# An attention and mixture-of-experts kernel: biased maxima in two halves of the heads, all first products beside the maxima, and a new order of residual, copy and norm

## What is computed

```python
# attention, per sequence: 32 heads of 8 dims
q, k, v = rope(x @ Wq.T), rope(x @ Wk.T), x @ Wv.T
gate = q . mean of k over each chunk of 32 tokens   # own chunk always, future chunks never
allowed = the 4 best chunks of each query, and causal
p = softmax(where(allowed, q.k * 8**-0.5, -1e30))
o = rmsnorm(p @ v) * o_norm_weight * sigmoid(x @ Wg1.T @ Wg2.T)
x = layernorm(x + o @ Wo.T)
# experts: 2 shared and 16 routed (4 chosen per token), 176 hidden features each
hidden = relu(x @ w1 + b1)
x = layernorm(x + x + sum_e gating_e * (hidden_e @ w2_e + b2_e))
```

## Time and profile before

| | |
|---|---|
| median of three runs | 1453.98 us |
| profiled execution, its own time | 1453.75 us |
| its span, first to last instruction | 1451.7 us |
| PE busy | 1332.4 us (92%) |
| DVE busy | 1087.7 us (75%) |
| ACT busy | 842.7 us (58%) |
| POOL busy | 533.9 us (37%) |
| mean granted clock of PE | 0.961 of full speed |

### The profile page before, as it was taken

One profiled execution on the slowest core, in us unless ns is written; L12 is line 12 of the kernel. 1 busy time (PEld: TensorE's weight loads), 2 busy tenths in 40 slices (PEclk: granted clock), 3 DMA queues, 4 the chain that ended last, 5 costly groups with the idle time before them and its releaser, 6 DMA issues.

```text
span 1451.7 us, 29057 instructions
## 1 busy us (share of the span) xinstructions
PE 1332.4 (92%) x10992; PEld 738.7 (51%) x10992; DVE 1087.7 (75%) x2747; ACT 842.7 (58%) x1266; POOL 533.9 (37%) x638
## 2 busy tenths in 40 slices
PE   5677999999998999999999999989999899999597
PEld 3422475535754366534755356543665347553364
DVE  6994688957897578966889578975889668885434
ACT  5406774396735876277743967358762877439121
POOL 3203542254323642245422553235432454225143
PEclk8667999999999999999999999999999999999799
DMA  6001022200321021210222003210112102220031
GB/s 243 16 15 17 16 79 76 52 17 16 104 66 38 30 59 60 74 31 16 82 71 55 16 17 102 71 33 30 60 62 71 31 16 68 73 53 23 13 113 58
DMA packets 52283, 77.81 MB, mean 54 GB/s; under 512 B 6334, under 2 KB 26800, under 8 KB 51888
## 3 DMA queue, kind: packets, MB, share of 16 engines
q1 hardware_dynamic: 52144, 75.96, 18.0%
HBM read 67.02 MB, written 8.65 MB: 52 GB/s over the span
## 4 chain that ended last, share of the span: by engine, by line
PE 61%; DVE 19%; ACT 11%; DVEq 3%; issue 3%; DMA 2%; POOL 1%; SPq 0%; POOLq 0%
PE PS L562 14%; PE PS L574 13%; PE PS L718 8%; ACT UQ L992 7%; PE PS L492 7%; PE PS L509 3%; DVE hr L1163 3%; ACT UK L992 2%; DVE CM L1356 2%; DVEq L1155 2%; PE PS L773 2%; PE PS L413 2%; DVE CM L1275 2%; PE PS L728 2%; PE PS L483 2%
## 5 line engine op out<-in xcount | busy, mean ns | idle before, releaser
L1051 POOL TENSOR_TENSOR hp<-hr,hp 128x512 f16<-128x512 f32 (+1 forms) x200 | 237.1, 1186 | 584.1 <-ACT hp L849 520.0
L1356 DVE TENSOR_REDUCE CM<-PS 128x32 f32<-128x1024 f32 x320 | 376.2, 1218 | 23.2 <-PE PS L492 18.9
L574 PE MATMUL PS<-W,hp 128*128 128x256 f16 (+1 forms) x2400 | 323.2, 274 | 4.6 <-POOL hp L1051 3.6
L562 PE MATMUL PS<-x1T,W 128*128 128x512 f16 (+1 forms) x1200 | 320.6, 385 | 0.0
L840 ACT ACTIVATE hr<-PS,CF 128x512 f32<-128x512 f32 (+1 forms) x200 | 137.2, 686 | 234.3 <-PE PS L562 234.3
L574 PEld LDWEIGHTS PS<-W,hp 128*128 128x128 f16 (+1 forms) x2400 | 216.9, 98 | 96.1 <-issue 34.7
L849 ACT ACTIVATE hp<-hr 128x512 f16<-128x512 f32 (+1 forms) x178 | 112.5, 632 | 169.3 <-DVE hr L1163 156.2
L1163 DVE TENSOR_TENSOR hr<-hr,gB 128x512 f32<-128x512 f32 x176 | 126.2, 717 | 64.9 <-ACT hr L840 58.5
L992 ACT ACTIVATE UK<-PS 128x1024 f32<-128x1024 f32 x160 | 153.0, 1037 | 11.4 <-PE PS L509 11.0
L562 PEld LDWEIGHTS PS<-x1T,W 128*128 128x128 f16 (+1 forms) x1200 | 107.7, 100 | 100.7 <-issue 34.9
L992 ACT ACTIVATE UQ<-PS 128x1024 f32<-128x1024 f32 x160 | 150.9, 1041 | 3.1 <-PE PS L509 1.4
(11 more groups left out here) (150 smaller groups left out, 1793.8 us busy)
## 6 DMA issues: line engine op xcount, KB each, us to landing
gB<-gates SPq DMA_DIRECT2D x64, 256.0 KB, 3.3
gB<-gates SPq DMA_DIRECT2D x32, 224.0 KB, 2.9
gB<-gates SPq DMA_DIRECT2D x32, 192.0 KB, 2.9
gB<-gates SPq DMA_DIRECT2D x32, 160.0 KB, 2.6
xT<-in_xT SPq DMA_DIRECT2D x8, 512.0 KB, 5.8
qET<-rows SPq DMA_DIRECT2D x16, 256.0 KB, 5.2
v<-in_x SPq DMA_DIRECT2D x8, 512.0 KB, 4.1
gB<-gates SPq DMA_DIRECT2D x32, 128.0 KB, 2.9
```

What stands on the lines that cost most here:

```text
L562: mm = pe.matmul(PS[0:w, BK_H[c % 2], :], W1[:, a, k, bass.ds(f0, w)], x1T[:, e, k, :], start=(n == 0), stop=(n == 5))
L574: mm = pe.matmul(PS[:, BK_Y + j // 2, (j % 2) * D:(j % 2 + 1) * D], hp[0:w, slot, a, j * P:(j + 1) * P], W2[0:w, e, bass.ds(c, 1), :].rear ...
L1051: nc.gpsimd.tensor_tensor(hp[0:w, slot, 1, :], hr[0:w, slot, :], hp[0:w, slot, 0, :], ALU.subtract).then_inc(pool_hp, 1)
L1356: nc.vector.tensor_reduce(dst, src, AX.X, ALU.max).then_inc(dve_cm, 1)
```

## The change

The biased maxima are computed in two halves of the heads. The first half (heads 0 to 15) is done within the maxima stage, behind units 21, 24, 27 and 30 (`FREE`). Its transposes stand behind the third up part of chunk 22, and SP's first half of `bias_rows` stands ahead of the gate broadcast of chunk 24. The second half is done after the maxima stage. Its transposes stand after key unit 8, its copy is made by DVE, and its rows are awaited ahead of key unit 20. All up parts (to chunk 24) are dealt beside the maxima, and so are the output gate's products, now in two calls whose operands stay on one row group each. The downs of chunk 22 (three parts), 23 and 24 stand among the first key units. Chunk 24's relu and high half go from ACT to DVE. The first ten key units use two pairs of banks. On DVE the residual sums, the copy of the outputs of group 0 and the whole norm follow in this order.

```diff
-C_FIRST, C_TOPK, C_MAX, C_BIAS = (0, 3), (3, 11), (11, 22), (22, 25)
+PAIRS = [n % 2 if n < 2 * NU else (2, 0, 1)[(n - 2 * NU) % 3] for n in range(TU)]
+BACK = [next((k for k in range(1, n + 1) if PAIRS[n - k] == PAIRS[n]), 0) for n in range(TU)]
+C_FIRST, C_TOPK, C_MAX, C_LATE = (0, 3), (3, 11), (11, 24), (24, 25)
-DEALT += [(MC - 2, 4), (MC - 2, 5), (MC - 2, 6)]
+DEALT += [(MC, 0), (MC, 1), (MC, 2)]
+AT_SEL, AT_GATE, AT_NEG = (1, 2), (3, 4), 11
+FREE = [u for u in range(TU // 2, MU) if all(part != 2 for _, part in dealt(u - 1))][0:2 * NT:2]
...
+            def bias_rows(b, n):                       # SP
+                pairs = slice(H // 4 * n, H // 4 * (n + 1))
+                if n == 0:
+                    sp.wait_ge(s_sel, 32 * (b + 1))
+                sp.wait_ge(pe_mx, b * TU + TU // 2 * (n + 1) + 1)
...
+                sp.wait_ge((act_neg, dve_neg)[n], b + 1)
...
+                    if m < B - 1 and c == NC - 1:      # in spread_gates
+                        bias_rows(m + 1, 0)
...
+                def gate_half(c, i):                   # PE
+                    r = ROW_G1 * i
+                    for j in range(2):
+                        mm = pe.matmul(PS[:, BK_H[(c + 1) % 2], j * D:(j + 1) * D], g1T[r:r + HD, j * P:(j + 1) * P],
+                                       WG2[r:r + HD, :], start=True, stop=True, tile_position=(r, 0))
+                def maxima_rows(bank, n):
+                    pe.wait_ge(dve_bias, (2 * b + n + 1) * NT)
+                    for j in range(NT):
+                        mm = pe.transpose(PS[0:HALF, bank, j * P:(j + 1) * P], negm[:, j, HALF * n:HALF * (n + 1)], ident)
...
+                    if n < RING:                       # in unit(g, d), n = g * NU + d
+                        pe.wait_ge(dve_cm, (b + 1) * TU + n + 1)
+                    if n == 2 * NU and m is not None:
                         pe.wait_ge(dve_z, 2 * m + 3)
+                    if n == TU // 2:
+                        pe.wait_ge(s_rows[1], 64 * (b + 1))
...
+                pe.wait_ge(s_rows[0], 64 * (b + 1))
+                unit(0, 0)
+                unit(0, 1)
+                late_down(NC - 3, (1,))
+                unit(0, 2)
+                late_down(NC - 3, (2, 3))
+                unit(0, 3)
+                late_down(NC - 2, (0, 1))
+                unit(0, 4)
+                late_down(NC - 2, (2, 3))
+                unit(1, 0)
+                outputs(0, 0, 0)
+                unit(1, 1)
+                late_down(NC - 1, (0, 1))
+                unit(1, 2)
+                outputs(0, 0, 1)
+                late_down(NC - 1, (2, 3))
+                unit(1, 3)
+                maxima_rows(BK_H[1], 1)
+                outputs(0, 0, 2)
+                unit(1, 4)
+                outputs(0, 0, 3)
...
+                        if u in FREE:                  # DVE, in the loop over the units
+                            maxima(FREE.index(u), 0)
+                if m is not None:
+                    dve.wait_ge(pe_h, m * NC + NC)
+                    nc.vector.tensor_scalar(hr[:, s_last, :], PS[:, BK_H[s_last], :], b1[:, NC - 1:NC], 0.0, ALU.add,
+                                            ALU.max).then_inc(s_hid, 1)
+                    gated(m, NC - 1, s_last, split=True)
                 for j in range(NT):
+                    maxima(j, 1)
+                dve.wait_ge(pe_neg, 2 * b + 2)
+                nc.vector.tensor_scalar(negT[:, 1, :], PS[0:HALF, BK_H[1], :], 1.0 / UNIT, None, ALU.mult).then_inc(dve_neg, 1)
...
                 if m is not None:
-                    finish(m, lambda: copy_outputs(0))
-                else:
-                    copy_outputs(0)
+                    residual(m)
+                copy_outputs(0)
+                if m is not None:
+                    finish(m)
```

More of the change, by code:

```diff
@@ L648, in turn @@
                 settled_wait(pe, dve_gm, (b + 1) * 3)
[L649 to L671, removed]
-                        down(m, c, c % 2, j)
[L674 to L705, removed]
+                for u in range(MU):
+                    if u == 1:
+                        pe.wait_ge(act_kz, (b + 1) * NG + 1)
+                        pe.wait_ge(act_eq, (b + 1) * NG + 1)
+                    pe.wait_ge(dve_cm, b * TU + u + 1)
+                    max_unit(u // NU, u % RING, u % NU)
+                    for cc, part in dealt(u):
+                        c = C_MAX[0] + cc
+                        if part == 0 and cc - 1 in AT_SEL:
+                            pe.wait_ge(act_sel, 2 * b + AT_SEL.index(cc - 1) + 1)
+                        if part == 0 and cc - 1 in AT_GATE:
+                            pe.wait_ge(act_eg, 2 * b + AT_GATE.index(cc - 1) + 1)
+                        if part == 0 and cc - 1 == AT_NEG:
+                            pe.wait_ge(act_neg, b + 1)
+                        if m is not None and part < 3:
+                            up(m, c, part)
+                        elif m is not None:
+                            down(m, c, c % 2, part - 3)
+                        if part == 2 and cc in AT_SEL:
+                            selection_rows(c, AT_SEL.index(cc))
+                        if part == 2 and cc in AT_GATE:
+                            gate_half(c, AT_GATE.index(cc))
+                        if part == 2 and cc == AT_NEG:
+                            if m is not None:
+                                pe.wait_ge(s_hid, m * NC + c + 2)
+                            maxima_rows(BK_H[(c + 1) % 2], 0)
@@ L942, in turn @@
                             high(m, c, (C_TOPK[0] + u) % 2)
[L943 to L953, removed]
@@ L1107, in causal @@
                     for n, t in enumerate(KORDER):
+                        if g == 0 and n == 1 and m is not None:
+                            for c in range(*C_LATE):
+                                low(m, c, c % 2)
                         if n != 2:
@@ L1191, in layernorm @@
                 inverse_root(NT)
-                if between is not None:
-                    between()
                 for j in range(NT):
```

133 lines of the change are left out of this document (70 added, 63 removed).

## The result

| | before | after |
|---|---|---|
| median | 1453.95 us (4 runs) | 1489.95 us (4 runs, 1487.41 to 1493.77) |
| ratio to before, 95% interval | | 1.0251 [1.0227, 1.0275] |
| span of the profiled execution | 1451.7 us | 1487.6 us |
| DVE busy | 1087.7 us | 1128.3 us |
| mean granted clock of PE | 0.961 | 0.958 |

The kernel is 36 us slower. The sign is as forecast, but 1463.5 was predicted and the range ended at 1475.

The account below looks back on a forecast made before the run. PE was taken to bound the maxima stage, DVE 4% behind, then ACT the keys. A turn: -11.5 + 8.0 + 1.3 + 4.3 = +2.1 us, seven +14.7, turn 0 -5.1: +9.6 on 1453.75, so 1463.5; range 1445 to 1475.

Parts of the forecast that it names:

- A: Between maxima and key stages: the late stage goes, first exponential at T + 0.43; 11.5 us less per turn.
- T: The moment at which PE leaves the maxima stage of a turn.
- B: PE's maxima stage: moved ups, downs, gate products and transposes add 8.0 us a turn, between 7.1 and 8.2.
- C: Second half of the maxima stage: DVE is 1.9 us too long, PE waits 1.3 a turn, between 0.3 and 2.3.
- a sum or reduction costs 0.16 + 0.001 per element: DVE's first-half maxima in the maxima stage: duration per operation, 3.6 us in all with the added drains.
- the forecast's own sum: Maxima stage, units 20 to 33: DVE 1.9 us too long, less about 0.6 that PE runs ahead; PE waits 1.3.
- D: Key stage: DVE's chain makes the copy of group 1 late; 4.3 us lost a turn, between 2.7 and 5.
- Both holes: Key stage: exponentials stop about 1.7 us by unit 10, for the residual sums, and 2.5 at unit 18.
- The clock: Rival: PE's clock falls after the new key-stage wait, 0.9 us each, at most 1.7; 1470 to 1476; chance 0.18.
- Turn 0: No experts, DVE bounds: first half adds 3.6 us, first exponential about 117.3 instead of 123.02; -5.1 us in all.

Follow-up runs that it names:

- run 7: The changed kernel without the scaled sums and reductions of the first half of the biased maxima, memsets in their place: 1464.88 us, ratio 1.0078.
- run 4: The kernel before with only DVE's order changed to residual sums, copy of group 0, whole norm: 1481.57 us, ratio 1.0191.

## Why the prediction was right in direction and wrong in size

- **A**, the late stage goes: right. First exponential at T + 0.43, 11.5 us.
- **B**, the work moved to PE: right. With DVE out of the way (run 7) the stage is 8.4 longer, forecast 8.0 with 8.2 as the upper bound. The gate's eight products took 2.1 us instead of the 1.06 of the earlier trace rows, with 1.9 forecast. The trace agrees with the case of one row group, and with the rule that the prediction cited from the Trainium skill ("TensorE: Matmul & The Clock Gate", section "The mechanism" of the packing part); no run alternates the row groups in the new place.
- **C**, DVE in the second half of the maxima stage: the step that failed. The place was right (PE waits behind units 24, 27, 30), the size was not: 1.3 forecast, at most 2.3, and 3.2 measured. The failing term is "a sum or reduction costs 0.16 + 0.001 per element". The earlier trace rows has that duration where POOL rests. In the new place each sum starts while POOL makes a low half, and takes 0.53 longer: 2.1 us a turn. With it the forecast's own sum gives 1.9 + 2.1 - 0.6 = 3.4. I had looked at DVE's and PE's totals and never laid POOL's timeline beside them, though both engines follow the same chunk. The trace of the kernel before had the sign, between the very rows that I took the duration from. DVE's and POOL's rows there:

```profile
789.48 0.46 DVE L1365 SCALAR_TENSOR_TENSOR rep<-cbias,CM 128x128 f32<-128x128 f16 x1 [0.44 <-issue]
...
793.43 1.19 DVE L1163 TENSOR_TENSOR hr<-hr,gB 128x512 f32<-128x512 f32 x1 [0.16 <-issue]
```

```profile
788.64 1.16 POOL L1051 TENSOR_TENSOR hp<-hr,hp 128x512 f16<-128x512 f32 x1 [4.16 <-ACT hp L849]
792.91 1.16 POOL L1051 TENSOR_TENSOR hp<-hr,hp 128x512 f16<-128x512 f32 x1 [3.12 <-ACT hp L849]
```

  The sum of 128 elements takes 0.46 beside POOL, where the same one takes 0.29 in turn 0, and the gating takes 1.19 instead of 0.68.
- **D**, the key stage: right in mechanism and nearly in size. Both holes are where they were forecast, and DVE's chain ends at T + 19.87. In part errors cancel in that: the copy of the second half is 0.8 late and the norm 0.4 shorter than forecast. And the first hole is mostly PE's own list (1.26 of 1.93), not the residual sums. In turn 7, where the clock does not fall, the stage takes 1381.36 - 1337.52 = 43.84, 5.0 more than before; forecast 4.3, upper bound 5. The holes are 1.93 + 2.17 = 4.1 of it, and 0.4 more is in the group behind the second one, where PE waits 0.61 for the next copy and five exponentials take 5.11 instead of 4.69.
- **The clock** was a rival at 0.18, an alternative to the forecast, with 0.9 a turn and 1.7 at most. It came on top of D in six turns of seven. Their key stages average 45.2, 1.3 over turn 7, and about 0.2 of this is the longer waits of turns 5 and 6. This was a fault of logic as well: D itself makes the wait of 2.5 us that the rival needs, so with D likely the clock's fall was likely too. The sum had the clock at nothing, and this is the second step that failed.
- **Turn 0**: -5.1 forecast, -2.0 without its earlier start. From first to last reduction DVE takes 54.5 us instead of 48.3: 6.2 more, where 3.6 was forecast. I had given the moved products no cost there since DVE bounds. But PE, with pauses, works there in part at the low clock (0.50 between 80 and 83 us). Its timeline has the second four gate products, and DVE's the reductions behind them:

```profile
80.74 2.07 PE L671 MATMUL PS<-WG,g1T 8*128 8x256 f32 x4
```

```profile
83.93 9.57 DVE L1394 TENSOR_REDUCE CM<-PS 128x32 f32<-128x1024 f32 x8 [1.85 <-PE PS L510]
```

  They take 2.07 instead of 1.12, DVE runs dry for 1.85, and its other waits in the stage sum to 1.7, where it had 0.49 before: 3.0 more. The halves themselves cost the other 3.2. That the slow products make the wait is read from the order of the rows; no run took them out.

A turn by these terms: -11.5 + 8.4 + 3.2 + 5.0 + 1.3 x 6/7 = +6.2, against 5.7 measured. The difference lies in the kernel before, which the terms take from its undisturbed turns. Its key stages of turns 1 and 3 are 0.9 longer than the others, at a clock of 0.96, and the late stage of turn 5 is 1.1 longer, since PE waits 1.58 for `negT` there and not 0.52. That is 2.9 us over seven turns, 0.4 each, which the kernel before loses too and the sum leaves out. The prediction took turn 4 for all turns, as repeating within 1 us; in fact they take 168.1 to 170.0.

The forecast was 26 us short. By these terms C is about 13 of it, the clock 8, D 5, B 3 and turn 0 less than 2, and those 3 us of the kernel before go the other way. Why turn 7 keeps its clock behind an equal wait of 2.47 stays open.

## What to carry to other kernels

When work is moved onto an engine that has room on average, lay the timelines of all engines over the new place, and look at what runs beside each moved operation. Here one unit's shift of four small sums was worth 14 us. An operation that is held up by another engine shows as a longer row, not as idle time, so a list of waits misses it: compare the durations of equal rows. A long chain of vector work should be cut where the matmul engine waits for something behind it. Here that gave back 22.6 of the 28.4 us that leaving the work out gives, and the clock was kept too. And a rival that the forecast's own mechanism sets off belongs in the sum, not beside it.

## What the runs showed of the hardware

A scaled sum on DVE with both inputs in SBUF (`cbias` and `CM`, L1378) does not get through its elements while POOL's subtraction runs. It took 0.89 us beside it and 0.36 behind it, for the same 192 elements. The four sums of the maxima stage end 0.09, 0.15, 0.21 and 0.28 us after POOL's operation, about 0.001 per element: only their start is hidden. The masks on POOL (L1137) hold a sum too. DVE's and POOL's rows behind T in turn 4:

```profile
816.14 1.23 DVE L1378 SCALAR_TENSOR_TENSOR rep<-cbias,CM 128x64 f32<-128x64 f16 x1
...
818.52 0.83 DVE L1378 SCALAR_TENSOR_TENSOR rep<-cbias,CM 128x192 f32<-128x192 f16 x1
```

```profile
816.14 1.16 POOL L1076 TENSOR_TENSOR hp<-hr,hp 128x512 f16<-128x512 f32 x1 [0.36 <-DVE hp L1193]
817.25 1.89 POOL L1137 TENSOR_SCALAR_AFFINE_SELECT UK<-UK 128x512 f32<-128x512 f32 x3
```

The sum of 64 elements takes 1.23 instead of 0.23, beside the subtraction. The one of 192 takes 0.83 and ends 0.21 behind the last mask. The sum of 128 between them takes 0.29, as alone, although POOL is at its masks then too. These two delays cost nothing, since DVE has 1.88 us idle behind them. DVE's reductions of PSUM (1.22 us each in the same stretch) do not lengthen. The Trainium skill states this in "SBUF — State Buffer", section "Who interferes with whom": a DVE instruction with two SBUF inputs contends with a GpSimd instruction that reads SBUF, and the one that comes second waits for the whole of the other. This trace agrees, with 0.53 us lost in each sum of the maxima stage. The prediction did not draw on it.

The fall of PE's clock behind a wait of about 2 us cost another 1.5 to 1.6 us of idle exponentials. With equal waits the holes are 3.12 against 1.60 (2.07 us, turns 6 and 4 of run 4) and 3.77 against 2.17 (2.47 us, turns 4 and 7 of the changed kernel). The length of the wait does not settle whether the clock falls: with 2.07 it fell in one turn and stayed in two, with 2.47 it fell in some turns of a run and stayed in others.
